# Maps of levels 1 and 2 kept in rows one element longer than the block row, and parity planes between the two levels

## The reference

```python
def basic_block(x, w1, w2, stride=1, ds=None):
    out = relu(conv3(x, w1, stride) * BN_S)
    out = conv3(out, w2, 1) * BN_S
    identity = conv1x1(x, ds, stride) * BN_S if ds is not None else x
    return relu(out + identity)

x = basic_block(x, e0b0c1, e0b0c2)                       # level 0, 64 x 64
x = basic_block(x, e0b1c1, e0b1c2);              f0 = x
x = basic_block(x, e1b0c1, e1b0c2, 2, e1b0ds)            # level 1, 32 x 32
x = basic_block(x, e1b1c1, e1b1c2);              f1 = x
x = basic_block(x, e2b0c1, e2b0c2, 2, e2b0ds)            # level 2, 16 x 16
x = basic_block(x, e2b1c1, e2b1c2)
x = (relu(deconv2(x, dec0w) * BN_S) + f1) * BN_S
x = (relu(deconv2(x, dec1w) * BN_S) + f0) * BN_S
```

## Time and profile before

| | us |
|---|---|
| median of 3 runs | 92.99 |
| lowest and highest | 92.93, 93.26 |
| the profiled execution | 93.48 |
| its span, first to last instruction | 91.3 |

### The profile page before, as it was taken

One profiled execution on the slowest core, in us unless ns is written; L12 is line 12 of the kernel. 1 busy time (PEld: TensorE's weight loads), 2 busy tenths in 40 slices (PEclk: granted clock), 3 DMA queues, 4 the chain that ended last, 5 costly groups with the idle time before them and its releaser, 6 DMA issues.

```text
span 91.3 us, 1542 instructions
## 1 busy us (share of the span) xinstructions
PE 83.4 (91%) x537; PEld 74.4 (81%) x537; DVE 63.1 (69%) x181; ACT 44.8 (49%) x94; POOL 28.0 (31%) x45
## 2 busy tenths in 40 slices
PE   5976999999999999999999999999999999998700
PEld 3764999998777799999977778999999999886500
DVE  5577999799858799556626479999368785343820
ACT  6006014778435066644513369899700399952300
POOL 7400060999920000743330001100990007000320
PEclk9999999999999999999999999999999999999955
DMA  2879810034681012640000000000000000000094
GB/s 31 251 215 321 288 71 0 7 115 125 149 268 63 2 43 83 215 119 6 0 0 0 0 4 0 0 0 0 7 0 0 0 0 4 7 0 0 14 327 118
DMA packets 4183, 6.51 MB, mean 71 GB/s; under 512 B 464, under 2 KB 2000, under 8 KB 4176
## 3 DMA queue, kind: packets, MB, share of 16 engines
q1 hardware_dynamic: 4176, 6.42, 23.0%
HBM read 5.37 MB, written 1.05 MB: 70 GB/s over the span
## 4 chain that ended last, share of the span: by engine, by line
PE 84%; DMA 6%; SPq 2%; ACT 2%; POOLq 1%; issue 1%; DVE 0%
PE psum L804 79%; DMA raw<-e0b0c_in 6%; PE psum L838 2%; PE psum L944 1%; SPq L412 1%; PE psum L1002 1%; POOLq L168 1%; ACT w_e0b0c L503 1%; PE psum L831 1%; SPq L416 0%; ACT shared L582 0%; ACT result L585 0%; DVE even L729 0%; PE psum L824 0%; POOLq L494 0%
## 5 line engine op out<-in xcount | busy, mean ns | idle before, releaser
L470 POOL TENSOR_TENSOR odd<-relu,odd 128x363 fp32r<-128x363 f32 x12 | 13.5, 1141 | 15.8 <-ACT odd L544 15.8
L804 PE MATMUL psum<-shared,w_e0b0c 128*128 128x364 f32 x72 | 12.5, 332 | 0.9 <-ACT w_e0b0c L503 0.9
L804 PEld LDWEIGHTS psum<-shared,w_e0b0c 128*128 128x128 f32 x72 | 11.9, 189 | 1.2 <-issue 1.1
L804 PE MATMUL psum<-shared,w_e0b1c 128*128 128x364 f32 x72 | 12.2, 329 | 0.0
L804 PEld LDWEIGHTS psum<-shared,w_e0b1c 128*128 128x128 f32 x72 | 12.1, 188 | 0.1
L804 PE MATMUL psum<-odd,w_e0b0c 128*128 128x512 f32 x48 | 11.9, 410 | 0.0
L804 PE MATMUL psum<-odd,w_e0b1c 128*128 128x512 f32 x48 | 11.9, 410 | 0.0
L720 DVE SCALAR_TENSOR_TENSOR relu<-psum,inside 128x363 f32<-128x363 f32 (+2 forms) x18 | 8.7, 491 | 3.7 <-PE psum L804 3.6
L804 PEld LDWEIGHTS psum<-odd,w_e0b1c 128*128 128x128 f32 x48 | 9.1, 190 | 2.5
L804 PEld LDWEIGHTS psum<-odd,w_e0b0c 128*128 128x128 f32 x48 | 9.1, 190 | 2.5
L544 ACT ACTIVATE odd<-relu 128x363 fp32r<-128x363 f32 x12 | 6.2, 519 | 7.4 <-DVE relu L720 7.4
(11 more groups left out here) (126 smaller groups left out, 140.4 us busy)
## 6 DMA issues: line engine op xcount, KB each, us to landing
out<-result SPq DMA_DIRECT2D x3, 256.0 KB, 3.1
x_sb<-x_in SPq DMA_DIRECT2D x4, 160.0 KB, 4.2
raw<-e0b0c_in SPq DMA_DIRECT2D x2, 256.0 KB, 5.3
raw<-e0b1c_in SPq DMA_DIRECT2D x2, 256.0 KB, 5.4
raw<-e1b1c_in SPq DMA_DIRECT2D x2, 256.0 KB, 2.9
raw<-e2b1c_in SPq DMA_DIRECT2D x2, 256.0 KB, 2.6
raw<-e1b0c_in SPq DMA_DIRECT2D x1, 448.0 KB, 3.7
raw<-e2b0c_in SPq DMA_DIRECT2D x1, 448.0 KB, 4.0
```

The lines of the kernel that those rows point to most:

```text
L470: pool.tensor_tensor(split_of(piece, 1), fp32_of(piece), split_of(piece, 0).bitcast(F32), ALU.subtract).then_inc(lo_ready, 1)
L804: last = pe.matmul(target, w, moving, start=(first and n == 0), stop=(final and n == len(terms) - 1), skip_group_check=skip)
```

## The change

All maps of levels 1 and 2 get rows of block row plus one: 17 at level 1, 9 at level 2. `odd1`, `odd2`, the corners and sides are plain runs (`RUN` = 290 and 82 for an image, `EVEN_RUN` = 272 and 72). The output of level 1 is no longer one map but four parity planes, `split1`, each of 8 rows of 9; `flat2` holds the maps of level 2. TensorE sums whole runs, and the elements between the rows are summed and left out when VectorE writes. e1b1c2 is therefore written by two high instructions (one for each row parity) and four low ones (one for each plane).

```diff
-FRONT = [2, 2, 1]
-EVEN_ROWS = [f + b + 1 for f, b in zip(FRONT, BLOCKS)]
-EVEN_COLS = [38, 22, 12]
-ODD_COLS = [BLOCKS[0] + 1, BLOCKS[1] + 1, BLOCKS[2] + 2]
+ODD_COLS = [b + 1 for b in BLOCKS]
+PITCH = [b + 1 for b in BLOCKS]
+MAP = [(b + 2) * (b + 1) + 2 for b in BLOCKS]
+RUN = [(b + 1) * (b + 1) + 1 for b in BLOCKS]
+EVEN_RUN = [b * (b + 1) for b in BLOCKS]
...
-        even = [None] + [sb(f"even{v}", [P, 2, IMAGES, EVEN_ROWS[v], EVEN_COLS[v]], F32R) for v in (1, 2)]
+        split1 = sb("split1", [P, 2, IMAGES, 2, 2, MAP[2]], F32R)
+        planes = [None, split0, split1]
+        flat2 = sb("flat2", [P, 2, IMAGES, MAP[2]], F32R)
+        flat = [None, flat1, flat2[:]]
+        odd2 = sb("odd2", [P, 2, IMAGES, RUN[2]], F32R)
+        corner2 = sb("corner2", [P, 2, IMAGES, EVEN_RUN[2]], F32R)
...
+        def sums_of(piece):
+
+            run = run_of(piece)
+            if STAGES[piece.stage].level == 2:
+                return bank_of(piece)[:, 0:IMAGES * run].rearrange("p (i n) -> p i n", i=IMAGES)
+            return bank_of(piece)[:, 0:run]
...
+        def side_copy(level, image, copy, run=None):
             side, to, start, count, (sy, sx) = copy
-                source = even[level - 1][start:start + count, :, image, f + sy:f + sy + 2 * ODD_ROWS[level] - 1:2,
-                                         f + sx:f + sx + 2 * ODD_COLS[level] - 1:2]
+            run = (0, RUN[level]) if run is None else run
+            first = sy // 2 * PITCH[level] + sx // 2
+            source = planes[level][start:start + count, :, image, sy % 2, sx % 2, first + run[0]:first + run[1]]
+            return sides[level][to:to + count, side, :, image, run[0]:run[1]], source.bitcast(F32)
...
@@ VectorE, the loop over the pieces @@
+                if stage.name == "e1b1c2":
+                    pairs = sums.rearrange("p (r a c) -> p a r c", a=2, c=PITCH[1])
+                    for i in range(2):
+                        last = dve.tensor_scalar(planes_inside(2, 0, image, i),
+                                                 pairs[:, i, :, 0:BLOCKS[1]].rearrange("p r (c b) -> p b r c", b=2),
+                                                 0.0, None, ALU.max)
+                    last.then_inc(hi_direct, 1)
+                    wait_half(dve, piece.index, 0)
+                    for i, j in [(0, 0), (0, 1), (1, 0), (1, 1)]:
+                        lo, hi = [plane_inside(2, half, image, i, j) for half in (1, 0)]
+                        last = dve.scalar_tensor_tensor(out=lo, in0=pairs[:, i, :, j:BLOCKS[1]:2], scalar=0.0,
+                                                        in1=hi.bitcast(F32), op0=ALU.max, op1=ALU.subtract)
+                    last.then_inc(lo_direct, 1)
+                elif stage.from_bank:
...
@@ TensorE @@
+            def of_images(maps, level, first, run, images):
+
+                runs = maps[:, :, first:first + run]
+                return runs if level == 2 else runs[:, images[0]]
...
                 def moving(half, s):
-                    if stage.name == "e1b0c1":
-                        sy, sx = s // shifts, s % shifts
-                        first = sy // 2 * PITCH_1 + sx // 2
-                        return split0[:, half, images[0], sy % 2, sx % 2, first:first + RUN_1]
...
-                    blocks = source[:, half, at, r:r + stride * (piece.rows - 1) + 1:stride,
-                                    c:c + stride * (cols - 1) + 1:stride]
-                    return blocks if len(images) > 1 else blocks[:, 0]
+                    sy, sx = s // shifts, s % shifts
+                    if stage.kind == "down":
+                        return of_images(planes[level][:, half, :, sy % 2, sx % 2], level,
+                                         sy // 2 * PITCH[level] + sx // 2, RUN[level], images)
...
+                    source, run = (odd, EVEN_RUN) if stage.kind == "even" else (flat, RUN)
+                    return of_images(source[level][:, half], level, sy * PITCH[level] + sx, run[level], images)
```

More of the change, by code:

```diff
@@ L271, in wait_w_lo, with lines_of @@
                 engine.wait_ge(w_lo, k)
-        def even_inside(level, half, images, row, rows):
-            f, b = FRONT[level], BLOCKS[level]
-            at = even[level][:, half, images[0]:images[-1] + 1, f + row:f + row + rows, f:f + b]
-            return at if len(images) > 1 else at[:, 0]
+        def lines_of(run, level):
+            return run.rearrange("p (r c) -> p r c", c=PITCH[level])[:, :, 0:BLOCKS[level]]
         def flat_inside(half, images, row, rows):
@@ new lines, in _ @@
+                if stage.name == "e1b1c2":
[12 more added lines that the diff above has]
+                elif stage.from_bank:
+                    if stage.level == 1:
+                        ins, his, los = [[lines_of(sums, 1)]] + [[map_inside(1, half, image)] for half in range(2)]
+                    else:
+                        ins = [lines_of(sums[:, one], 2) for one in range(IMAGES)]
+                        his, los = [[map_inside(2, half, one) for one in range(IMAGES)] for half in range(2)]
+                    if stage.level == 1:
+                        dve.tensor_scalar(his[0], ins[0], 0.0, None, ALU.max).then_inc(hi_direct, 1)
+                    else:
+                        every = sums.rearrange("p i (r c) -> p i r c", c=PITCH[2])[:, :, :, 0:BLOCKS[2]]
+                        dve.tensor_scalar(maps_inside(2, 0), every, 0.0, None, ALU.max).then_inc(hi_direct, 1)
+                    wait_half(dve, piece.index, 0)
+                    for one in range(len(ins)):
+                        last = dve.scalar_tensor_tensor(out=los[one], in0=ins[one], scalar=0.0,
+                                                        in1=his[one].bitcast(F32), op0=ALU.max, op1=ALU.subtract)
+                    last.then_inc(lo_direct, 1)
@@ L878, in _ @@
                         pe.wait_ge(eye_ready, 1)
-                    terms = [(eye_r[:], flat1_inside(half, images[0]) if level == 1 else
-                              even_inside(level, half, images, piece.row, piece.rows)) for half in range(2)]
+                    terms = [(eye_r[:], of_images(flat[level][:, half], level, PITCH[level] + 1, EVEN_RUN[level], images))
+                             for half in range(2)]
                 elif stage.shortcut is not None:
@@ L960, in _ @@
                     for side in range(2):
-                        hi, lo = [sides[level][:, side, half, at] for half in range(2)]
-                        if len(images) == 1:
-                            hi, lo = hi[:, 0], lo[:, 0]
+                        hi, lo = [of_images(sides[level][:, side, half], level, 0, RUN[level], images)
+                                  for half in range(2)]
                         n = len(WHOLE) + side
```

218 lines of the change are left out of this document (93 added, 125 removed).

## The result

| | before | changed |
|---|---|---|
| median of 12 runs each, us | 93.17 (92.73 to 93.62) | 92.46 (92.18 to 92.77) |
| ratio, with its 95% interval | | 0.9917 (0.9899 to 0.9936) |
| profiled execution, us | 93.48 | 92.77 |
| its span, us | 91.3 | 91.0 |

The changed kernel is faster by 0.7 us, where 0.31 us was forecast. About half of that lies in the span and comes close to the sum. The rest lies where no term looked: in the time around the span. The kernel before has 93.17 us in these twelve runs; the forecast started from its 92.99 us, the median of three.

The account below looks back on a forecast made before the run. TensorE, busy nearly throughout at full clock, was taken as the bound. Terms -0.23 (sides), -0.04 and -0.04 sum to -0.31 us: profiled 93.48 to 93.17, median 92.99 to 92.68 us; range 92.2 to 93.25.

Parts of the forecast that it names:

- change of the stage: From level 1 through level 2: -0.23 us at the sides, then -0.04 and -0.04, together -0.31 us.
- The new wait: Image 1's sums of e1b1c2 ready at 73.05 us, VectorE free only at 73.28; TensorE's five start at 73.83, not 73.67.
- ScalarE was late next: Ahead of e2b0c1's sides: TensorE ready at 75.51 us, ScalarE's copies done at 75.65, sides start at 75.70, gaining 0.23.
- Rival 2: Between image 0's low half and image 1's sides: non-overlapping VectorE writes delay ScalarE's side copies; 93.51 us, chance 0.12.
- The step of two: In e2b0c1's ten matmuls, reading every second element costs 0.055 us each; neighbouring runs take 0.11 instead of 0.166 us.
- Level 1: Second half: 48 matmuls read 272 columns in one run, 0.004 us less each; image 1's e1b1c2 ends 0.14 us earlier.
- A break of the row: In level 1's matmuls, reading 256 columns in 16 rows instead of one run costs 0.011 us.
- rival 3: Level 1's padding costs more than broken rows, 93.2 us; other half: the ten stay at 0.166, 93.05 us; chance 0.10.
- Rival 1: In level 2, all 36 late matmuls take 0.103 us: -0.3 instead of -0.04, giving 92.35 us; chance 0.20.
- three corner copies of VectorE: Ahead of level 2's shortcut: end at about 76.25 us, hidden under the six side matmuls, which last until 76.36.
- 2.2 us lie around the span: Outside the span: profiled execution 93.48 us, span 91.3 us; the difference was worked out on the execution and subtracted from the median.

Follow-up runs that it names:

- two-write kernel: The changed kernel with each half of e1b1c2 written by VectorE in one instruction of 256, planes cleared in one, level 2's input wrong: 92.43 us, ratio 0.992.
- the one with POOL's corners: The changed kernel with image 0's four corner copies on POOL, one side more on ScalarE and one less on VectorE: 92.31 us, ratio 0.9907.

## Why the prediction was right, and where it was not

The range held the result and the chain of waits was the one predicted, but the closeness of the median owes something to luck: the base of 92.99 us was 0.18 us under the twelve-run median, and the gain forecast was 0.40 us too small. The prediction gave the largest chance to a gain too small to be told from none, and the measured one is clear of the noise.

The predicted steps are set against the trace after, as it stands and less the 0.10 us by which that trace reaches level 1 later:

| step | predicted | measured | less 0.10 |
|---|---|---|---|
| 12 of 272 columns | 1.52 | 1.51 | |
| image 0's sums | 71.27 | 71.31 | 71.21 |
| two high writes, four low | 0.50, 0.64 | 0.49, 0.62 | |
| image 1's high half starts | 73.28 | 73.26 | 73.16 |
| ten matmuls start | 74.41 | 74.39 | 74.29 |
| ScalarE's nine copies end | 75.65 | 75.59 | 75.49 |
| sides start | 75.70 | 75.64 | 75.54 |
| e2b0c2 starts | 76.94 | 76.96 | 76.86 |
| change of the stage | -0.31 | -0.38 | |

- **The new wait** for VectorE came where and as large as worked out (image 1's five at 73.81, predicted 73.83). ScalarE was late next, as predicted, but by half: 0.09 us where 75.70 - 75.51 = 0.19 was worked out. TensorE could have begun the sides at 75.55, 0.11 us behind the start of the last of the ten (75.44 in the trace), and began at 75.64. The two-write kernel and the one with POOL's corners, which take waits of this chain away, gained 0.25 and 0.27 us of the stage.
- **Rival 2** (ScalarE or small VectorE writes make it slower) failed on the term named as decisive: four 64-element writes took 0.62 us, not 1.16.
- **The step of two** was the largest term and right in kind: putting it back costs 0.19 us in the stage and 0.29 at the sides. Of the 0.055 us for a matmul the step itself is 0.039.
- **Level 1** had the right sign for a wrong reason. "A break of the row (0.011 us for 16 rows)" costs some 0.003 us; rows of 16 at a pitch of 17 took 0.125 us and the run of 272 took 0.126. The gain was 0.005 for a matmul instead of 0.004, and it belongs to what `odd1` of before was, not to runs. From the first matmul of e1b0c1 to the first of e2b0c1 it came to 0.22 us (72.99 - 56.50 before, 72.87 - 56.60 after), where the sum had 0.14. The first half of rival 3, that the padding costs more than the breaks that it avoids, is what the shortcut shows (some 0.005 against 0.003 us); it did not make level 1 slower, since the new `odd1`, in rows too, took 0.006 us less for a matmul than the one of before (0.125 against 0.131). Its other half failed: the ten went from 0.166 to 0.111 us.
- **Two misses cancelled** in the stage. The sides started 0.39 us earlier (less the 0.10 us), where 0.23 was predicted; from the sides to the end of the stage the kernel lost 0.01 us (8.40 us before, 8.41 after), where 0.08 was to be gained.
- **Rival 1** (36 late matmuls at 0.103) was wrong: the groups of 144 columns go at the floor as before, of the twelve of e2b0c2 the last lasts 0.28 us and the first is followed at 0.17, which leaves (1.56 - 0.28 - 0.17) / 10 = 0.111 us. After the sides the changed kernel even lost time: sides and shortcut start to the fillers took 1.15 us (75.64 to 76.79) against 0.97, since the first matmuls behind a wait come late and, it seems, since the three corner copies of VectorE end only at 76.16 (the prediction had them hidden, and with the corners done at 75.83 in the kernel with two writes the shortcut group took 0.33 us instead of 0.37); of these 0.18 us, 0.12 came back in the next wait (76.79 to 76.96, where before had 76.90 to 77.19).
- **The step that failed** is not in the sum of the stages but in how it was carried to the run: "2.2 us lie around the span", taken as if the change could not touch it. It fell to 1.77 us with POOL's program two instructions shorter. This 0.42 us is more than the layouts brought (0.34), and both kernels show it: give either the other's POOL count and it takes the other's time around the span. The measured median, 92.46, is 0.22 us under the forecast, and -0.7 us is 0.3 in the span and 0.4 around it. Why the length of POOL's program acts on this time stays open.

## What to carry to other kernels

Compare time less span before anything else: if it differs between two kernels, that part of the difference isn't in any engine's row, and a few instructions more or less on one engine can make it as large as the change itself. Before a cost is put down to a shape, look for a row that has the shape without the cost; here the identity matmuls had broken rows at 0.125 us and would have shown that rows weren't what made 0.131. And when copies for one consumer are spread over engines, follow each engine's queue to its last copy: the ten matmuls that became 0.5 us faster (1.66 us to 1.16 without the wait) gave only as much as the slowest of these queues allowed.

## What the runs showed of the hardware

- **Time around the span goes with the length of POOL's program, up and down.** By POOL's records in the trace (with waits and semaphores): 54 gave 1.75 us, 56 1.78, 58 1.77 to 1.79 (four kernels, two different programs of POOL), 59 1.99 and 2.00 (two), 60 2.17 to 2.20 (three, two programs), 62 1.79, 63 1.94. Equal counts gave equal times in kernels with different work and spans. One more instruction on VectorE did nothing (60 on POOL, 2.17). Why 62 is short again, and whether the time lies ahead of the first instruction or behind the last, stays open: the trace shows neither.
- **A floor for matmuls of few columns.** Groups with weights of 128 columns started 0.111 us apart at 164 columns, as at 180 and 128 before; above it, one run of 256 columns took 0.120 us, of 272 0.125 to 0.126, of 290 0.135. The Trainium skill's page "TensorE: Matmul & The Clock Gate", section "Back-to-back issue gap", makes the gap of a single matmul columns at 2.4 GHz plus a few ns, 116 ns for 272, and gives about 81 ns at 128 columns for a stream of matmuls with their weight loads. The trace shows 10 ns more at 272 and 30 ns more at 128; for 16 more columns in one run the trace has 5 to 6 ns where the formula has 7.
- **The first matmuls behind a wait come late.** The six of the sides, which start behind a wait, took 0.78 us to the shortcut group, against 0.66 before, where TensorE itself came last. The twelve of e2b0c2 start behind a wait in both kernels, and there the second follows the first at 0.17 us, the others at 0.111.
- **What `odd1`'s pitch of 18 cost**, 0.131 against 0.125 us for the same 16 rows of 16, has no cause here.
